# Layer 0 of a two-layer model: the products with C of four of sixteen states made by GpSimd instead of VectorE

## The chip, the cores and the metric
One core of a Trainium2 chip. The time is the device time of one execution, in microseconds.

## What is computed
Two layers on a batch of 8 sequences of 1024 tokens with 256 channels. The change lies in layer 0, in the selective scan of its Mamba block, inner width 512, 16 states:

```
def step(h, xs):
    d_t, B_t, C_t, u_t = xs
    dA = jnp.exp(d_t[..., None] * A)
    dBu = d_t[..., None] * B_t[:, None, :] * u_t[..., None]
    h = dA * h + dBu
    y_t = jnp.einsum('bdn,bn->bd', h, C_t)
    return (h, y_t)
...
y = _selective_scan(xm, delta, A, Bm, Cm, Dp)      # y + u * Dp
y = y * _silu(res)
return y @ out_proj_w.T
```

Around it stand the projection in, a convolution over four tokens, the projection out, an MLP and a mixture of experts. Layer 1 (attention with a memory term, and an MLP) is not touched.

## The kernel before
The kernel is written by hand: each engine has its own list of instructions, which it takes in order, and semaphores tie the lists. A sequence is worked in two half-sequences of 512 tokens, `j` = 0 to 15. The 512 inner channels are four tiles of 128 partitions, in two pairs `e`. For each pair the sixteen states `n` are passed, and for each state the two tiles `d`. One such (state, tile) is a step `k`: 64 steps in a half-sequence, 1024 in all; a group `g` is the two steps of one state.

In each step ScalarE writes the decay, exp(delta * A), into one of four PSUM banks (`state_bank(k)`, line 1374). GpSimd writes `drive` = delta * u * B for both tiles of a group at once (L1789), in one of three slots. VectorE scans over the 512 tokens, in place in the bank (L1578), and one scan later multiplies the states with C into `heavy` (L1560, in `weigh`). TensorE adds this piece to the y accumulators in PSUM by four transposes of 128x128 (L1056, in `add_y`). B and C of a state come by DMA over SyncE's queue (L874), spread to all partitions, into one of four slots of `bc_wide`. Four semaphores tell how far each is: `decay_done`, `driven`, `scanned`, `weighed`, and `piece_added` that a slot of `heavy` (six of them, `W_SLOTS`) is free again. A bank is written anew when its product is made; in the first half of a sequence ScalarE saves the last column to `carry` first, with which the second half starts.

At the begin of each pair VectorE multiplies the finished accumulators of the pair before with the gate (`gate_pair`, L1568), and GpSimd makes two pieces x * D into `heavy` (L1796).

Between the steps TensorE does the side work, which is everything else of layer 0 for the half-sequence after and those before: `xt` (transposes of x, L962), `xm` (projection in, L968), `cv` (convolution, L975), `res` (L981), `xd` (L986), `dl` (L991), `yt` (L996), `m` (projection out, L1002), `h` and `o` (MLP, L1007 and L1012 to L1016). A planner, `side_times`, gives each unit a step on TensorE (`PE_AT`), and its drain a step on ScalarE some six steps after the unit's end (`ACT_AT`, `put(ACT_AT, _to + 6, _unit)`) or, for `o` and two small sums, on VectorE (`DVE_AT`). The units share two PSUM banks in turn (`SIDE_BANKS`), so a unit waits until the unit two before it is drained. ScalarE's drain at step s stands behind its decay of step s - 1, and that decay waits for the product of step s - 5. On TensorE a unit of step k stands ahead of the piece of step k.

Of the kernel before, what the change touches and what calls it, by code (L numbers as in the profile page):

```python
# [15 lines left out]
ALU = mybir.AluOpType  # L16
# [106 lines left out]
W_SLOTS = 6  # L123
# [10 lines left out]

def piece_of(j, e, u, d):

    return ((j * ND + e) * (NS + 1) + u) * MD + d
# [416 lines left out]
def build(nc, x_in, w_in, p_in, moe1_in, moe2_in, resid, out):  # L554
    ctx = ExitStack()
    with ctx:
# [23 lines left out]
        def param(name):  # L580
# [7 lines left out]
        bc_wide, drive, heavy, after_scan = place(  # L588
            arena_at, ("bc_wide", [P, BC_SLOTS, 2, HALF]), ("drive", [P, DRIVE_SLOTS, MD, HALF]),
            ("heavy", [P, W_SLOTS, HALF]))  # L590
# [103 lines left out]
        piece_added = sem("piece_added")  # L694
        y_gated = sem("y_gated")
# [131 lines left out]
        def _(sp):  # L827
# [38 lines left out]
            for g in range(NH * GROUPS):  # L866
                for task in SP_AT.get(g, ()):
                    row_task(task)
                j, n = g // GROUPS, g % NS
                if g >= BC_SLOTS:  # L870
                    sp.wait_ge(driven, g - BC_SLOTS + 1)
                    sp.wait_ge(weighed, MD * (g - BC_SLOTS + 1))
                sp.wait_ge(bc_saved, 16 * (j + 1))
                sp.dma_start(bc_wide[:, g % BC_SLOTS, :, :], bc_dram[j, n:n + 1].broadcast_to([P, 2, HALF]))\  # L874
                  .then_inc(bc_in[g % BC_SLOTS], 16)
# [66 lines left out]
        def _(pe):  # L942
# [117 lines left out]

            for k in range(NH * STEPS):
                j, e, n, d = k // STEPS, k // (NS * MD) % ND, k // MD % NS, k % MD
                for unit in PE_AT.get(k, ()):
                    side(unit)
                if n == 0 and d == 0:
                    if k:
                        pe.wait_ge(y_gated, TC * (j * ND + e))
                    for i in range(MD):
                        pe.wait_ge(skip_done, (j * ND + e) * MD + i + 1)
                        add_y(j, e, 0, i)  # L1070
                pe.wait_ge(weighed, k + 1)
                add_y(j, e, n + 1, d)
# [175 lines left out]
        def _(act):  # L1248
# [112 lines left out]
            for k in range(NH * STEPS):  # L1361
                j, e, n, d = k // STEPS, k // (NS * MD) % ND, k // MD % NS, k % MD
                for task in ACT_AT.get(k, ()):
                    task_of(task)
                if n == 0 and d == 0 and e == 0:
                    act.wait_ge(softplus_done, j + 1)
                if k >= banks:
                    old = k - banks
                    act.wait_ge(weighed, old + 1)
                    if old // STEPS % NC == 0:  # L1370
                        f(carry[:, old // (NS * MD) % ND, old // MD % NS, old % MD:old % MD + 1],
                          state_bank(old)[:, HALF - 1:HALF], ACT.Copy).then_inc(carried, 1)
                        act.wait_ge(carried, old // (NC * STEPS) * STEPS + old % STEPS + 1)
                f(state_bank(k), delta[j % 2][:, e * MD + d, :], ACT.Exp,
                  scale=neg_a[:, (e * MD + d) * NS + n:(e * MD + d) * NS + n + 1]).then_inc(decay_done, 1)
# [85 lines left out]
        def _(dve):  # L1461
# [101 lines left out]
            def gate_pair(j, e):  # L1563
                dve.wait_ge(piece_added, piece_of(j, e + 1, 0, 0))
                dve.wait_ge(gate_silu, j + 1)
# [4 lines left out]
            for k in range(NH * STEPS):  # L1570
# [7 lines left out]
                V.tensor_tensor_scan(state_bank(k), state_bank(k), drive[:, g % DRIVE_SLOTS, d, :],  # L1578
# [4 lines left out]
                if k:  # L1583
                    weigh(k - 1)
# [174 lines left out]
        def _(pool):  # L1759
# [18 lines left out]

            for e in range(ND):
                row_task(("du", 0, e))  # L1780
            for g in range(NH * GROUPS):
                j, e, n = g // GROUPS, g // NS % ND, g % NS
                for task in POOL_AT.get(g, ()):
                    row_task(task)
# [153 lines left out]
```

## Time and profile before
| | us |
|---|---|
| three timed runs | 4795.88, 4803.9, 4829.52; median 4803.9 |
| profiled execution | 4818.0, its span 4815.0 |
| first scan of layer 0 to the last | 185.8 to 2320.0 in the span |
| busy in the span: TensorE, VectorE | 4237.4, 3286.6 |
| busy in the span: ScalarE, GpSimd | 2585.4, 1925.5 |

A busy time is the time in which at least one instruction of the engine is shown running. Shares over the whole span mix layer 0's prelude, its scans and layer 1, which have different limits; only the stretch from 185.8 to 2320.0 has the code of the change.

### The profile page before, as it was taken

The page shows a single profiled execution, that of the slowest core. Times are in us where ns is not written, and L with a number is a line of the kernel's source. Part 1 is how long each engine was busy: PE and PEld are TensorE (multiplying, and loading weights), DVE is VectorE, ACT ScalarE, POOL GpSimd, SP SyncE. Part 2 cuts the span into 40 slices and gives each one's busy share as a digit, 9 for nine tenths or more (in the row PEclk, how much of TensorE's full clock was granted, in tenths as well). Part 3 has the DMA queues.
Part 4 walks back from the last instruction along what each step waited for, and adds up shares of the span by engine and source line. Part 5 has one row for each costly group of instructions (what it writes and reads, how often), then busy time and mean ns, then how long its engine had stood idle before and what let it go on. Part 6 is the DMA issues. An engine that isn't in the chain of part 4 may idle for free.

```text
span 4815.0 us, 59412 instructions
## 1 busy us (share of the span) xinstructions
PE 4237.4 (88%) x20448; PEld 2458.1 (51%) x20448; DVE 3286.6 (68%) x4828; ACT 2585.4 (54%) x4047; POOL 1925.5 (40%) x1545
## 2 busy tenths in 40 slices
PE   8878888888888888887679999999999999999997
PEld 4544555555555555555444545544555445545444
DVE  0498999898999989899364564746547465564643
ACT  3465757666776767676224444444454444444444
POOL 0366666666666666666221211313122131221311
PEclk9968899898989999998779989999899989989899
DMA  2233334343433434343211121211212112121111
GB/s 95 93 131 131 122 134 144 128 149 127 149 137 127 153 124 148 132 138 136 88 38 30 21 55 21 39 33 25 48 25 51 21 28 48 22 49 26 22 39 23
DMA packets 156684, 391.58 MB, mean 81 GB/s; under 512 B 22676, under 2 KB 77284, under 8 KB 155748
## 3 DMA queue, kind: packets, MB, share of 16 engines
q1 hardware_dynamic: 156388, 387.79, 26.6%
q8 instruction: 166, 2.72, 0.2%
q14 instruction: 130, 1.06, 0.1%
HBM read 316.06 MB, written 18.87 MB: 70 GB/s over the span
## 4 chain that ended last, share of the span: by engine, by line
PE 62%; DVE 18%; ACT 9%; issue 8%; DMA 1%; POOL 1%; SPq 0%; DVEq 0%; ACTq 0%; POOLq 0%
DVE ps L1578 10%; PE ps L1135 7%; PE ps L1117 6%; PE ps L1235 5%; PE ps L1095 5%; PE ps L1228 5%; PE ps L1056 4%; DVE heavy L1560 3%; ACT L1250 3%; PE ps L1007 3%; PE ps L1160 2%; PE ps L981 2%; PE ps L1099 2%; PE ps L1166 2%; PE ps L991 2%
## 5 line engine op out<-in xcount | busy, mean ns | idle before, releaser
L1789 POOL TENSOR_TENSOR drive<-du,bc_wide 128x1024 f32<-128x1024 f32 x512 | 1207.0, 2364 | 668.2 <-DMA bc_wide<-bc_dram 560.7
L1610 DVE TENSOR_REDUCE smax<-ps 128x2 f32<-128x1024 f32 (+3 forms) x768 | 733.9, 956 | 547.2 <-PE ps L1099 369.9
L1250 ACT ACTIVATE exps<-ps 128x1024 f32<-128x1024 f32 (+3 forms) x768 | 621.0, 810 | 710.4 <-PE ps L1117 706.9
L1250 ACT ACTIVATE ps<-delta,neg_a 128x512 f32<-128x512 f32 x1024 | 701.0, 690 | 315.4 <-DVE heavy L1560 299.3
L1818 POOL TENSOR_SCALAR_AFFINE_SELECT exps<-exps 128x256 f32<-128x256 f32 x512 | 214.3, 421 | 1386.8 <-ACT exps L1250 1385.6
L1056 PEld LDWEIGHTS ps<-p_all,heavy 128*128 128x128 f32 x4352 | 552.7, 152 | 386.2 <-issue 189.6
L1056 PE MATMUL ps<-p_all,heavy 128*128 128x128 f32 x4352 | 648.7, 295 | 98.3 <-DVE heavy L1560 63.6
L1578 DVE TENSOR_TENSOR_SCAN ps<-ps,carry,drive 128x512 f32<-128x512 f32 x512 | 655.9, 1281 | 80.9 <-ACT ps L1250 80.3
L1560 DVE TENSOR_TENSOR heavy<-bc_wide,ps 128x512 f32<-128x512 f32 x1024 | 691.1, 675 | 17.8 <-PE ps L1056 17.5
L1578 DVE TENSOR_TENSOR_SCAN ps<-ps,drive 128x512 f32<-128x512 f32 x512 | 623.4, 1218 | 65.4 <-ACT ps L1250 49.8
L1095 PE MATMUL ps<-ks,qs 64*128 64x512 f32 (+3 forms) x1536 | 337.1, 436 | 79.9 <-DVE smax L1610 62.9
L1135 PE MATMUL ps<-exps,vals 128*32 128x512 f32 (+3 forms) x3072 | 385.6, 542 | 7.3 <-ACT exps L1250 3.1
L1117 PE MATMUL ps<-qs,ks 64*128 64x512 f32 (+3 forms) x1536 | 352.0, 456 | 32.7 <-ACT exps L1250 29.0
L1117 PEld LDWEIGHTS ps<-qs,ks 64*128 64x128 f32 x1536 | 152.8, 196 | 327.0 <-ACT exps L1250 143.1
L1095 PEld LDWEIGHTS ps<-ks,qs 64*128 64x128 f32 x1536 | 153.4, 196 | 315.2 <-DVE smax L1610 127.4
L1250 ACT ACT_TABLE_LOAD x235 | 301.5, 1283 | 5.0 <-PEq L1931 0.8
L1007 PE MATMUL ps<-mT,w_mlp 128*128 128x512 f32 x512 | 248.3, 610 | 56.9 <-ACT mT L1250 43.6
L1250 ACT ACTIVATE h<-ps,p_all 128x512 f32<-128x512 f32 x256 | 174.6, 682 | 202.9 <-PE ps L1228 170.1
L1016 PE MATMUL ps<-w_mlp,h 128*128 128x256 f32 x1024 | 258.3, 410 | 5.5 <-ACT h L1250 5.5
L1235 PE MATMUL ps<-g,h 128*128 128x256 f32 x1024 | 261.3, 413 | 0.0
L1228 PE MATMUL ps<-xT,g 128*128 128x512 f32 x512 | 251.9, 614 | 0.0
L975 PE MATMUL ps<-raw,taps 128*128 128x512 f32 x512 | 230.4, 592 | 0.0
(176 smaller groups left out, 5580.4 us busy)
## 6 DMA issues: line engine op xcount, KB each, us to landing
bc_wide<-bc_dram SPq DMA_DIRECT2D x512, 512.0 KB, 3.6
qs<-q_hi SPq DMA_DIRECT2D x256, 64.0 KB
ks<-k_hi SPq DMA_DIRECT2D x256, 64.0 KB, 2.4
x_row<-in_x SPq DMA_DIRECT2D x15, 1024.0 KB, 7.4
resid<-mix SPq DMA_DIRECT2D x9, 1024.0 KB, 6.8
x_row<-resid SPq DMA_DIRECT2D x9, 1024.0 KB, 5.5
xn<-resid SPq DMA_DIRECT2D x8, 1024.0 KB, 5.4
qs<-q_lo SPq DMA_DIRECT2D x128, 64.0 KB
```

Source lines behind the costliest of these rows:

```text
L1007: last = mm(bank, w_up0[:, k, m * P:(m + 1) * P], mT[:, k, :], start=(k == 0), stop=(k == KD - 1))
L1056: last = mm(acc_tile(t)[:, d * P:(d + 1) * P], heavy[:, slot, t * P:(t + 1) * P], ident, is_transpose=True, start=(u == 0 and d == 0 and t ...
L1095: last = mm(both[:, i * HALF:i * HALF + n], qs[head, slot, it * P:(it + 1) * P], ks[head, slot, ch * HALF:ch * HALF + n], start=True, stop ...
L1117: last = mm(both[:, i * HALF:i * HALF + n], ks[head, slot, jt * P:(jt + 1) * P], qs[head, slot, at:at + n], start=True, stop=True, skip_gr ...
L1135: last = mm(ps[tile:tile + VP, PV_BANK, HALF - n:], vals[:, b % 2, first:first + VP], exps[:, at + i * n:at + (i + 1) * n], start=jt < 2, ...
L1228: last = mm(bank, g1[:, k, m * P:(m + 1) * P], xT[:, b % 2, k, tokens(TC * c, HALF)], start=(k == 0), stop=(k == KD - 1))
L1235: last = mm(bank[:, 0:D], h1[:, m, tt * P:(tt + 1) * P], g2[:, m, :], start=(m == 0), stop=(m == MF - 1))
L1250: return nc.scalar.activation(out_, in_, func, **kw)
L1560: V.tensor_tensor(heavy[:, piece % W_SLOTS, :], bc_wide[:, g % BC_SLOTS, 1, :], state_bank(k), ALU.mult).then_inc(weighed, 1)
L1578: V.tensor_tensor_scan(state_bank(k), state_bank(k), drive[:, g % DRIVE_SLOTS, d, :], carry[:, e, n, d:d + 1] if j % NC else 0.0, ALU.mult ...
L1610: V.tensor_reduce(into, both, AX_X, ALU.max).then_inc(drained_v, 1)
L1789: G.tensor_tensor(drive[:, g % DRIVE_SLOTS, :, :], du[j % 2][:, e * MD:(e + 1) * MD, :], wide(bc_wide[:, g % BC_SLOTS, 0, :], MD), ALU.mul ...
```

## The change
The states n = 0, 4, 8 and 12 of each pair (`POOL_STATES`) are scanned out of the decay's bank into a buffer in SBUF, `held`, which has room for the two tiles of one state. GpSimd multiplies both tiles with C in place, by one instruction of 128x1024 (`weigh_held`), ahead of the drive of the third state after. In a sequence's first half it also copies the two last columns to `carry`, which ScalarE did. TensorE adds the eight transposes of `held` after the sixth step of each eight (`add_held`, at d = 1 of state n + 2). The scan of the next kept state waits until that is done (`held_added`). ScalarE may write a kept state's bank anew as soon as it is scanned, not weighed. SyncE waits for `held_weighed` before it overwrites such a state's C. `heavy` has four slots instead of six, which makes room for `held`; `piece_of` and `weighs_to` count the pieces and products that are left.

```diff
-W_SLOTS = 6
+W_SLOTS = 4
+POOL_STATES = (0, 4, 8, 12)
...
+            def add_held(j, e, n):
+
+                pe.wait_ge(held_weighed, pool_group(j, e, n) + 1)
+                for d in range(MD):
+                    for t in range(TC):
+                        last = mm(acc_tile(t)[:, d * P:(d + 1) * P], held[:, d, t * P:(t + 1) * P], ident,
+                                  is_transpose=True, start=False, stop=False, skip_group_check=True)
+                last.then_inc(held_added, 1)
...
-                pe.wait_ge(weighed, k + 1)
-                add_y(j, e, n + 1, d)
+                if not by_pool(n):
+                    pe.wait_ge(weighed, weighs_to(k) + 1)
+                    add_y(j, e, n + 1, d)
+                if d == MD - 1 and n >= 2 and by_pool(n - 2):
+                    add_held(j, e, n - 2)
...
-                    act.wait_ge(weighed, old + 1)
-                    if old // STEPS % NC == 0:
+                    if by_pool(old // MD % NS):
+                        act.wait_ge(scanned, old + 1)
+                    else:
+                        act.wait_ge(weighed, weighs_to(old) + 1)
+                    if old // STEPS % NC == 0 and not by_pool(old // MD % NS):
...
+                if by_pool(n) and d == 0:
+                    if pool_group(j, e, n):
+                        dve.wait_ge(held_added, pool_group(j, e, n))
+                    if j % NC:
+                        dve.wait_ge(held_carried, (j // NC * ND + e) * len(POOL_STATES) + POOL_STATES.index(n) + 1)
-                V.tensor_tensor_scan(state_bank(k), state_bank(k), drive[:, g % DRIVE_SLOTS, d, :],
+                V.tensor_tensor_scan(held[:, d, :] if by_pool(n) else state_bank(k), state_bank(k), drive[:, g % DRIVE_SLOTS, d, :],
                                      carry[:, e, n, d:d + 1] if j % NC else 0.0, ALU.mult, ALU.add)\
                     .then_inc(scanned, 1)
...
-                if k:
+                if k and not by_pool((k - 1) // MD % NS):
                     weigh(k - 1)
...
+            def weigh_held(g):
+
+                j, e, n = g // GROUPS, g // NS % ND, g % NS
+                pool.wait_ge(scanned, MD * (g + 1))
+                if j % NC == 0:
+                    G.tensor_copy(carry[:, e, n, :], held[:, :, HALF - 1]).then_inc(held_carried, 1)
+                    pool.wait_ge(held_carried, (j // NC * ND + e) * len(POOL_STATES) + POOL_STATES.index(n) + 1)
+                G.tensor_tensor(held[:, :, :], held[:, :, :], wide(bc_wide[:, g % BC_SLOTS, 1, :], MD), ALU.mult)\
+                    .then_inc(held_weighed, 1)
...
+                if g >= DRIVE_SLOTS and by_pool((g - DRIVE_SLOTS) % NS):
+                    weigh_held(g - DRIVE_SLOTS)
```

In the lists of instructions below the scan is shown as SCALAR_TENSOR_TENSOR, and in brackets stand the semaphores that an instruction waits for. VectorE around the second kept state (n = 4) of the first pair, before:

```order
L1578 SCALAR_TENSOR_TENSOR ps<-ps,drive 128x512 [waits decay_done,driven]
L1560 TENSOR_TENSOR heavy<-bc_wide,ps 128x512 [waits scanned]
L1578 SCALAR_TENSOR_TENSOR ps<-ps,drive 128x512 [waits decay_done]
L1560 TENSOR_TENSOR heavy<-bc_wide,ps 128x512 [waits piece_added,scanned]
L1578 SCALAR_TENSOR_TENSOR ps<-ps,drive 128x512 [waits decay_done,driven]
```

The same place now:

```order
L1600 TENSOR_TENSOR heavy<-bc_wide,ps 128x512 [waits piece_added,scanned]
L1624 SCALAR_TENSOR_TENSOR held<-ps,drive 128x512 [waits held_added,decay_done,driven]
L1600 TENSOR_TENSOR heavy<-bc_wide,ps 128x512 [waits scanned]
L1624 SCALAR_TENSOR_TENSOR held<-ps,drive 128x512 [waits decay_done]
L1624 SCALAR_TENSOR_TENSOR ps<-ps,drive 128x512 [waits decay_done,driven]
L1624 SCALAR_TENSOR_TENSOR ps<-ps,drive 128x512 [waits decay_done]
L1600 TENSOR_TENSOR heavy<-bc_wide,ps 128x512 [waits piece_added,scanned]
```

Two products are gone behind the two scans into `held`, and the first of these scans has one more semaphore to wait for.

TensorE in the second pair of a half-sequence, from the second `m` unit (L1002, now L1027) to the third `h` unit (L1007, now L1032) and the one after, before:

```order
L1002 MATMUL ps<-yT,w_l_52 128x512 x4
L1056 MATMUL ps<-p_all,heavy 128x128 x12
L1007 MATMUL ps<-mT,w_mlp_53 128x512 x2
L1056 MATMUL ps<-p_all,heavy 128x128 x8
L1007 MATMUL ps<-mT,w_mlp_53 128x512 x2
L1056 MATMUL ps<-p_all,heavy 128x128 x4
L1020 MATMUL ps<-row_mv,p_all 128x1
L1007 MATMUL ps<-mT,w_mlp_53 128x512 x2
L1056 MATMUL ps<-p_all,heavy 128x128 x4
L1007 MATMUL ps<-mT,w_mlp_53 128x512 x2
```

The same place now, from the kept state before it:

```order
L1091 MATMUL ps<-p_all,held 128x128 x8
L1081 MATMUL ps<-p_all,heavy 128x128 x4
L1027 MATMUL ps<-yT,w_l_53 128x512 x4
L1081 MATMUL ps<-p_all,heavy 128x128 x4
L1032 MATMUL ps<-mT,w_mlp_54 128x512 x2
L1081 MATMUL ps<-p_all,heavy 128x128 x8
L1032 MATMUL ps<-mT,w_mlp_54 128x512 x2
L1081 MATMUL ps<-p_all,heavy 128x128 x4
L1045 MATMUL ps<-row_mv,p_all 128x1
L1032 MATMUL ps<-mT,w_mlp_54 128x512 x2
L1081 MATMUL ps<-p_all,heavy 128x128 x4
L1091 MATMUL ps<-p_all,held 128x128 x8
```

The eight transposes of the kept state stand behind three `h` units and behind the transposes of the sixth step of the block.

GpSimd in the second half of a sequence, now; before, only the drives stood there:

```order
L1847 TENSOR_TENSOR drive<-du_80,bc_wide 128x1024 [waits scanned,bc_in1,du_done]
L1847 TENSOR_TENSOR drive<-du_80,bc_wide 128x1024 [waits scanned,bc_in2,du_done]
L1832 TENSOR_TENSOR held<-held,bc_wide 128x1024 [waits scanned]
L1847 TENSOR_TENSOR drive<-du_80,bc_wide 128x1024 [waits scanned,bc_in3,du_done]
L1847 TENSOR_TENSOR drive<-du_80,bc_wide 128x1024 [waits scanned,bc_in0,du_done]
```

The product of the kept state stands ahead of the drive of the third state after it, and every fifth large instruction is now such a product.

## Rows read from the trace of the kernel before

**Rows 1.** Groups by line and form, whole trace: count, busy us, mean ns, idle before.
```profile
L1560 DVE TENSOR_TENSOR heavy<-bc_wide,ps 128x512 f32<-128x512 f32 x1024 | 691.1, 675 | 17.8 <-PE ps L1056 17.5
...
L1578 DVE TENSOR_TENSOR_SCAN ps<-ps,carry,drive 128x512 f32<-128x512 f32 x512 | 655.9, 1281 | 80.9 <-ACT ps L1250 80.3 <-POOL drive L1789 0.2
...
L1789 POOL TENSOR_TENSOR drive<-du,bc_wide 128x1024 f32<-128x1024 f32 x512 | 1207.0, 2364 | 668.2 <-DMA bc_wide<-bc_dram 560.7 <-DVE ps L1578 84.2 <-issue 22.9
...
L1705 DVE TENSOR_TENSOR_SCAN gsum<-p_all,gsum,ps 112x512 f32<-112x512 f32 x48 | 61.5, 1281 | 2.1
```

**Rows 2.** Waits of VectorE from 300 to 2300 us: total us, times, longest.
```profile
DVE ps L1578 <- ACT ps L1250: 124.2, 77, 5.0
DVE heavy L1560 <- PE ps L1056: 17.5, 27, 1.8
```

**Rows 3.** Windows over the eight blocks of half-sequence 7, all engines.
```profile
1124.83:1145.20 20.37, 13.48 (x65) 10.10 (x64) 16.04 (x22) 15.30 (x22) 13.73 (x7) 0.75 0.35 121
1145.20:1160.46 15.26, 15.26 (x67) 8.89 (x66) 14.45 (x17) 8.86 (x15) 9.45 (x4) 1.00 0.58 203
1160.46:1176.58 16.12, 11.85 (x58) 7.19 (x56) 14.31 (x17) 11.12 (x14) 9.46 (x4) 1.00 0.40 135
1176.58:1194.76 18.18, 17.71 (x81) 12.53 (x82) 14.97 (x18) 13.30 (x19) 8.54 (x4) 0.91 0.34 117
1194.76:1212.36 17.60, 16.09 (x88) 11.99 (x86) 16.65 (x24) 6.47 (x10) 12.58 (x7) 1.00 0.28 100
1212.36:1231.64 19.28, 16.01 (x52) 9.73 (x52) 15.31 (x20) 12.56 (x16) 10.85 (x6) 0.73 0.38 131
1231.64:1246.41 14.77, 12.51 (x54) 7.22 (x53) 14.77 (x19) 6.96 (x11) 11.37 (x6) 1.00 0.35 120
1246.41:1261.44 15.03, 13.23 (x57) 7.65 (x56) 15.03 (x21) 9.47 (x14) 10.61 (x5) 1.00 0.41 138
```

**Rows 4.** Timeline of block 7, half-sequence 7: start us, duration us, engine, line, [idle before].
```profile
1240.49 0.67 DVE L1560 TENSOR_TENSOR heavy<-bc_wide,ps 128x512 f32<-128x512 f32 x1
...
1241.82 0.58 ACT L1250 ACTIVATE mT<-ps 128x512 f32<-128x512 f32 x1
...
1242.54 1.95 PE L1007 MATMUL ps<-mT,w_mlp 128*128 128x512 f32 x4 [2.26 <-ACT mT L1250]
...
1245.82 0.67 DVE L1560 TENSOR_TENSOR heavy<-bc_wide,ps 128x512 f32<-128x512 f32 x1
...
1246.41 1.28 DVE L1578 TENSOR_TENSOR_SCAN ps<-ps,carry,drive 128x512 f32<-128x512 f32 x1
...
1249.70 0.60 PE L1056 MATMUL ps<-p_all,heavy 128*128 128x128 f32 x4
```

**Rows 5.** Timeline of block 3, half-sequence 7.
```profile
1176.58 1.29 DVE L1578 TENSOR_TENSOR_SCAN ps<-ps,carry,drive 128x512 f32<-128x512 f32 x1 [1.81 <-ACT ps L1250]
...
1177.05 1.12 PE L996 MATMUL ps<-p_all,gate 128*128 128x128 f32 x4 [1.86 <-ACT yT L1250]
...
1183.30 0.60 PE L1056 MATMUL ps<-p_all,heavy 128*128 128x128 f32 x4
```

**Rows 6.** Timeline of TensorE in blocks 1, 6, 8 and the half-sequence after.
```profile
1150.52 1.04 PE L1056 MATMUL ps<-p_all,heavy 128*128 128x128 f32 x8
...
1216.39 1.12 PE L991 MATMUL ps<-xd_rows,w_l 64*128 64x512 f32 x2 [3.23 <-DVE mix L1503]
...
1234.06 1.48 PE L1056 MATMUL ps<-p_all,heavy 128*128 128x128 f32 x12
...
1263.30 1.91 PE L1056 MATMUL ps<-p_all,heavy 128*128 128x128 f32 x16
...
1275.07 3.30 PE L968 MATMUL ps<-xT,w_l 128*128 128x512 f32 x4 [4.66 <-ACT raw L1250]
```

**Rows 7.** Windows, columns as in 3: all of half-sequence 8.
```profile
1261.44:1392.40 130.96, 114.11 (x493) 72.49 (x492) 122.28 (x166) 100.29 (x186) 91.39 (x43) 0.92 0.43 145
```

**Rows 8.** Windows, columns as in 3: first to last scan of layer 0.
```profile
185.80:2320.00 2134.20, 1788.66 (x7648) 1142.43 (x7648) 1939.44 (x2465) 1419.32 (x2332) 1405.35 (x633) 0.88 0.39 136
```

More of the change, by code:

```diff
@@ L132, in group_of, with by_pool, pool_group, weighs_to @@
     return (j * ND + e) * NS + n
+def by_pool(n):
+    return n in POOL_STATES
+def pool_group(j, e, n):
+    return (j * ND + e) * len(POOL_STATES) + POOL_STATES.index(n)
+def weighs_to(k):
+    pairs, n, d = k // (NS * MD), k // MD % NS, k % MD
+    return (pairs * (NS - len(POOL_STATES)) + n - sum(m < n for m in POOL_STATES)) * MD + (0 if by_pool(n) else d)
 def piece_of(j, e, u, d):
-    return ((j * ND + e) * (NS + 1) + u) * MD + d
+    n = u - sum(m + 1 < u for m in POOL_STATES)
+    return ((j * ND + e) * (NS + 1 - len(POOL_STATES)) + n) * MD + d
 def side_units(i):
@@ L587, in build @@
         L0_COLS = W_AT["qk"][0]
-        bc_wide, drive, heavy, after_scan = place(
+        bc_wide, drive, heavy, held, after_scan = place(
             arena_at, ("bc_wide", [P, BC_SLOTS, 2, HALF]), ("drive", [P, DRIVE_SLOTS, MD, HALF]),
-            ("heavy", [P, W_SLOTS, HALF]))
+            ("heavy", [P, W_SLOTS, HALF]), ("held", [P, MD, HALF]))
         (w_l0, w_mlp0, taps, neg_a, ew_sum, ln_stats, ln_mv, ln_rstd, ln_shift, row_stats, row_mv, row_q, carry, tail,
@@ L694, in build @@
         piece_added = sem("piece_added")
+        held_weighed = sem("held_weighed")
+        held_carried = sem("held_carried")
+        held_added = sem("held_added")
         y_gated = sem("y_gated")
@@ L870, in _ @@
                 if g >= BC_SLOTS:
-                    sp.wait_ge(driven, g - BC_SLOTS + 1)
-                    sp.wait_ge(weighed, MD * (g - BC_SLOTS + 1))
+                    old = g - BC_SLOTS
+                    sp.wait_ge(driven, old + 1)
+                    if by_pool(old % NS):
+                        sp.wait_ge(held_weighed, pool_group(old // GROUPS, old // NS % ND, old % NS) + 1)
+                    else:
+                        sp.wait_ge(weighed, weighs_to(MD * (old + 1)))
                 sp.wait_ge(bc_saved, 16 * (j + 1))
@@ L1368, in _ @@
                     old = k - banks
-                    act.wait_ge(weighed, old + 1)
-                    if old // STEPS % NC == 0:
+                    if by_pool(old // MD % NS):
+                        act.wait_ge(scanned, old + 1)
+                    else:
+                        act.wait_ge(weighed, weighs_to(old) + 1)
+                    if old // STEPS % NC == 0 and not by_pool(old // MD % NS):
                         f(carry[:, old // (NS * MD) % ND, old // MD % NS, old % MD:old % MD + 1],
                           state_bank(old)[:, HALF - 1:HALF], ACT.Copy).then_inc(carried, 1)
-                        act.wait_ge(carried, old // (NC * STEPS) * STEPS + old % STEPS + 1)
+                        act.wait_ge(carried, old // (NC * STEPS) * weighs_to(STEPS) + weighs_to(old % STEPS) + 1)
                 f(state_bank(k), delta[j % 2][:, e * MD + d, :], ACT.Exp,
@@ L1564, in gate_pair @@
                 dve.wait_ge(piece_added, piece_of(j, e + 1, 0, 0))
+                dve.wait_ge(held_added, len(POOL_STATES) * (j * ND + e + 1))
                 dve.wait_ge(gate_silu, j + 1)
```

## The prediction

> **What bounds the kernel now.** Read the whole-trace groups first, then the windows of layer 0, then VectorE's waits, and last the order of time inside one block of steps. Layer 0's scan part lasts 2134.2 us of the span and VectorE is busy 1939.4 of it, TensorE 1788.7, GpSimd 1405.4 [rows 8]. It is VectorE that sets the pace: a scan of 1281 ns and a product of 675 ns per step, pipelined, 1024 times [rows 1]. It waits 124.2 us for ScalarE's decays and only 17.5 us for TensorE [rows 2]. So a product taken from VectorE looks like time gained.
>
> The second thing to see is how far TensorE runs behind VectorE, and why. Number the steps of a half-sequence 0 to 63 (two tiles per state, sixteen states, two pairs) and cut them into eight blocks of eight; each block begins with a state that the change gives to GpSimd. At the end of block 7 VectorE starts the first scan of block 8 at 1246.41. The transposes of step 53 (the sixth of block 7) end at 1249.70 + 0.60 = 1250.30 [rows 4]: TensorE is 3.9 us late against that scan. This lag is not a heap of old work. TensorE had sat idle for 2.26 us until 1242.54, waiting for ScalarE to drain mT; the drain at 1241.82 stands behind the decay that needed the product started at 1240.49 [rows 4]. The side work (convolution, projections, MLP) uses two banks in turn, and its drains are tied to ScalarE's place in the steps, which is tied to VectorE's. At present this costs nothing, since six pieces may wait in heavy. Block 3 shows the same: idle 1.86 us before 1177.05 for yT, step 21 ended at 1183.90, while the first scan of block 4 began at 1176.58, 7.3 us earlier [rows 5].
>
> **The change part by part.** (1) Removed from VectorE: 256 products. A product takes the engine 0.59 us from start to start (1245.82 to the scan at 1246.41, [rows 4]), so a block gets 1.19 us shorter on VectorE's side and all 128 blocks 151 us. The Trainium skill (VectorE: DVE Perf Modes, "The DRAIN you can't avoid") says that the next operation does not start until the pipe has emptied; here the scan starts before the 0.67 us product has ended, so the measured 0.59 stands. By that rule the saving would be 256 times the mean 675 ns, 173 us.
>
> (2) The scans of the kept states write SBUF instead of PSUM. The scan of layer 1 that reads PSUM and writes SBUF, 512 elements, takes 1281 ns, as the one here does [rows 1]: taken at nothing, between 0 and the 0.06 us by which the two groups of scans might differ, 512 times, 30 us at most either way.
>
> (3) Added to GpSimd: 256 products of 128x1024. The form stands in the trace as drive, 2364 ns [rows 1]: 605 us. For half of them a copy of 128x2 as well, not in the trace; above nothing and below a quarter of that operation, 0 to 0.6 us each, taken at 0.2: 26 us. GpSimd is idle for 2134.2 - 1405.4 = 729 us there [rows 8], so it fits, with 98 us to spare. The product is issued ahead of the drive three states later, so it delays that drive by 2.4 us, and it frees its bc_wide slot for SyncE's queue, which stands behind it. The kept product comes about 2.4 us after its scans, while TensorE asks for it after five more steps; I take no wait from this.
>
> (4) TensorE: as many transposes as before. Eight of a kept state come at once behind the sixth step of the block, 1.04 us by the row of eight [rows 6].
>
> (5) The new wait, the one that decides. There is one held buffer. The first scan of a block waits until TensorE has added the kept state of the block before, and in TensorE's queue those eight transposes stand behind the sixth step's side work and transposes. Behind the waiting scan are all scans and products of VectorE; ScalarE's decays and GpSimd's drives wait for those. So a block cannot be shorter than: the time from its first scan to the end of its sixth step on TensorE, plus 1.04 for the eight transposes, plus 0.1 for two semaphores, less the 1.19 by which VectorE reaches the releasing point earlier. That is 0.05 less than the distance measured now. It holds where a wait inside the block made TensorE late, since then nothing is inherited; where TensorE was late from an earlier block the wait itself has cleared that, and I take VectorE's own time, the block less 1.19.
>
> The eight blocks of half-sequence 7 last 20.37, 15.26, 16.12, 18.18, 17.60, 19.28, 14.77 and 15.03 us, 136.6 in all [rows 3]. Block by block, after:
> - Block 3: 1183.90 - 1160.46 = 23.4 in place of 16.1 [rows 3, 5].
> - Block 6: TensorE idles 3.23 us for VectorE's mix, then works partly at 1.2 GHz, the lower of its two levels (the granted clock of the block is 0.73 on average); step 45's transposes end at 1234.06 + 1.04 = 1235.10, so 22.7 in place of 19.3 [rows 3, 6].
> - Block 7: 1250.30 - 1231.64, 18.6 in place of 14.8 [rows 3, 4].
> - Block 8: step 61 ends at 1263.30 + 1.04 = 1264.34, 17.9 in place of 15.0 [rows 3, 6].
> - Block 1: step 5 ends at 1150.52 + 0.60 = 1151.1, 26.2 us after the block's begin, against 19.2 by VectorE alone [rows 3, 6]. Part of this lag comes from the Gelu, which would start earlier once TensorE hands over a shorter queue. I take 22, nearer the low end, for 20.4 now.
> - Block 2: TensorE is busy all of its 15.26 us, with inherited work [rows 3]; I take 15.0.
> - Blocks 4 and 5 by VectorE's own time: 17.0 and 16.4 [rows 3].
> Sum 153.0 against 136.6, 16.4 more. Half-sequence 8 (131.0 us, [rows 7]) belongs to the other kind, in which the next sequence is normalised; there TensorE idles 4.66 us for raw in block 1 [rows 6], the same pattern, and I take 16 for it as well. The first and the last half-sequence have little side work: there VectorE's own gain stands, 8 times 1.19, 9.5 each. In all 14 times 16 less 19, 205 us. The profiled execution took 4818 us, which makes 5023; it was 14 above the median of the three timed runs, so against 4804 I say **5009 us**, 4% slower.
>
> heavy with four slots in place of six adds nothing to this: the product that would wait for a slot needs a step that the held wait has asked for already, or one that TensorE finishes early in the block. Alone it would cost, since the lag of 3.9 to 7.3 us above is more than a window of two states.
>
> **The rivals.** Rival A, faster: the lag is old work and TensorE catches up as soon as VectorE asks. Then a block lasts the longer of VectorE's own time and TensorE's busy time: 19.2, 15.3, 14.9, 17.7, 16.4, 18.1, 13.6, 13.8 [rows 3], 129.0, so 7.6 less per half-sequence and 122 in all: 4682 us. It speaks for it that TensorE is busy for 1788.7 of 2134.2 us only [rows 8]; against it are the idle stretches of 1.9 to 4.7 us right ahead of the late steps [rows 4 to 6]. It decides once TensorE has its sixth step done within 0.7 us of its product, which is what the two steps of VectorE that follow (1.78 us) leave beside 1.04 us of transposes.
>
> Rival B, GpSimd's products are what TensorE and the drives wait for: then of the 151 us all but a little is given back, and GpSimd, with 98 us to spare over 128 blocks, stalls VectorE in the blocks that also hold du and the joins. At one product's 2.36 us in each of 64 blocks, 151 us, this comes out level: 4804 us. Against it is that a drive is ready early in most blocks and GpSimd idles before it.
>
> Rival C, no lag is cleared: each block lasts as long as the distance measured now, inherited work included. Blocks 2 and 4 would show the lags of blocks 1 and 3 again, some 4 us each, and block 1 its 26.2: 12 more per half-sequence, 168 in all, 5177 us.
>
> Rival D, the change does not do what it says, the wait being met by an earlier release. The order shows TensorE's eight transposes behind the sixth step in every block, so I leave it little.
>
> **How the numbers follow.** Forecast 0.72, from 4883 (the lag counts for less than half: 14 times 7 less 19 is 79) to 5121 (block 1 at its upper end and 4 us more in block 2: 14 times 24 less 19 is 317); rival A 0.06; rival B and D together 0.12, 4780 to 4880; rival C 0.10. The range of 4860 to 5130 leaves out A, most of B and C. Within 1% is about what a measurement of this kernel can tell from no change, that is 4756 to 4852: 0.08. Faster 0.06, slower 0.86.
>
> **What would show it.** Right: the scans into held wait for TensorE's transposes of held, over 300 us in total, in blocks 1, 3, 6, 7 and 8, hardly in 5; ScalarE's stalls of VectorE shrink below 124 us; TensorE's idle waits for ScalarE's drains grow; the products and scans keep 675 and 1281 ns; layer 1 is unchanged. Wrong: held waits below 100 us (A), or waits of TensorE for held_weighed and of scans for drive (B). The forecast would fail most easily through the assumption that ScalarE's drains come no earlier relative to the steps than they do now.

## The result, and the profile after

The changed kernel takes **5038.8 us** (median of 4 runs, 5034.0 to 5055.0), the kernel before 4810.6 in the same session (4 runs, 4795.9 to 4829.5): a ratio of 1.048, 95% interval 1.043 to 1.052. The forecast was 5009 us, with a range of 4860 to 5130. The profiled execution has a span of 5037.9 us.

First the windows: the scan part of layer 0 (first scan to last) and the stretch of layer 1 from its first to its last gate scan, of the kernel after and then of the kernel before. (The first window of the kernel after runs to the end of its last scan, 1.3 us more than to its start.) Columns: window, length, busy time and count of TensorE, its weight loads, VectorE, ScalarE and GpSimd, granted clock, DMA share, GB/s.

```profile
186.80:2577.40 2390.60, 1877.86 (x7642) 1184.44 (x7643) 1785.49 (x2209) 1392.88 (x2204) 1708.03 (x825) 0.85 0.36 122
2728.60:4778.60 2050.00, 1939.05 (x10651) 1026.70 (x10649) 1189.28 (x2060) 958.17 (x1405) 442.85 (x795) 0.92 0.17 33
```
```profile
185.80:2318.70 2132.90, 1787.55 (x7644) 1141.71 (x7644) 1938.14 (x2464) 1419.32 (x2332) 1405.35 (x633) 0.88 0.39 137
2473.50:4559.40 2085.90, 1965.28 (x10669) 1037.71 (x10667) 1187.97 (x2061) 961.38 (x1409) 448.20 (x798) 0.91 0.17 33
```

VectorE did lose its work: 1785 us busy, 153 fewer. And yet layer 0's scan part is longer, 2389.3 us from first to last scan start against 2132.9, **256.4 more**. Layer 1 gives 36 of it back in this pair of profiles, but nothing there was changed: over the fourteen traces of this study, one of each kernel, that stretch lasts from 2043 to 2094 us. It goes with TensorE's granted clock in it: the two longest (2094 and 2086, the second that of the kernel before) have 0.901 and 0.909, the two shortest (2043 and 2050, the second that of the kernel after) 0.927 and 0.921. What sets that clock is open, and so is how much of the 36 us belongs to the kernels and how much to these two executions. A difference in the whole time of some 25 us can lie outside the changed code, so the lengths of the scan part are given below where it matters.

Next the costliest groups, with the idle time of the engine ahead of each; they answer to [rows 1].

```profile
L1600 DVE TENSOR_TENSOR heavy<-bc_wide,ps 128x512 f32<-128x512 f32 x768 | 516.0, 672 | 145.5 <-PE ps L1081 145.1
L1624 DVE TENSOR_TENSOR_SCAN held<-ps,carry,drive 128x512 f32<-128x512 f32 x128 | 163.6, 1278 | 202.2 <-PE ps L1091 190.0 <-POOL drive L1847 10.6 <-ACT ps L1287 1.6
L1624 DVE TENSOR_TENSOR_SCAN held<-ps,drive 128x512 f32<-128x512 f32 x128 | 155.8, 1218 | 170.4 <-PE ps L1091 156.3 <-POOL drive L1847 12.6 <-ACT ps L1287 1.3
L1832 POOL TENSOR_TENSOR held<-held,bc_wide 128x1024 f32<-128x1024 f32 x128 | 301.2, 2353 | 174.3 <-DVE held L1624 169.1
L1847 POOL TENSOR_TENSOR drive<-du,bc_wide 128x1024 f32<-128x1024 f32 x512 | 1203.9, 2359 | 333.9 <-DMA bc_wide<-bc_dram 137.6 <-issue 134.8 <-DVE ps L1624 57.0
L1830 POOL COPY carry<-held 128x2 f32<-128x2 f32 x64 | 12.0, 187 | 122.0 <-DVE held L1624 121.9
```

The durations are what they were: 672 ns a product, 1278 ns a scan, also into SBUF; GpSimd's new product takes 2353 ns. The idle time is new: 346 us ahead of scans into `held`, for the transposes of the kept state (L1091; this is called the held wait below), and 145 us ahead of VectorE's own products, for those of pieces (L1081). ([rows 2] had 17.5 of the latter.)

The eight blocks of half-sequence 7, to be laid beside [rows 3]:

```profile
1225.55:1248.14 22.59, 16.18 (x75) 11.10 (x73) 14.65 (x19) 14.61 (x20) 16.66 (x9) 0.85 0.41 140
1248.14:1262.02 13.88, 13.88 (x59) 7.88 (x57) 13.10 (x14) 7.28 (x12) 10.59 (x5) 1.00 0.44 147
1262.02:1285.31 23.29, 15.53 (x64) 9.77 (x62) 13.21 (x15) 13.51 (x18) 14.27 (x7) 0.78 0.27 93
1285.31:1300.62 15.31, 14.73 (x80) 11.51 (x78) 13.43 (x15) 11.20 (x14) 8.51 (x4) 1.00 0.37 137
1300.62:1319.18 18.56, 14.70 (x66) 10.11 (x64) 15.53 (x22) 5.96 (x9) 17.04 (x9) 0.82 0.32 118
1319.18:1339.63 20.45, 18.46 (x70) 11.24 (x70) 14.18 (x17) 12.24 (x15) 12.72 (x6) 0.83 0.31 103
1339.63:1361.16 21.53, 15.51 (x53) 8.56 (x50) 13.85 (x16) 7.74 (x12) 16.21 (x7) 0.84 0.28 98
1361.16:1380.14 18.98, 14.57 (x57) 8.36 (x58) 13.54 (x18) 11.22 (x16) 8.42 (x4) 0.91 0.32 111
```

And block 7 in order of time (start, duration, engine, line, idle before), to be laid beside [rows 4]:

```profile
1339.63 1.28 DVE L1624 TENSOR_TENSOR_SCAN held<-ps,carry,drive 128x512 f32<-128x512 f32 x1 [3.84 <-PE ps L1091]
...
1347.28 0.67 DVE L1600 TENSOR_TENSOR heavy<-bc_wide,ps 128x512 f32<-128x512 f32 x1
...
1348.61 0.58 ACT L1287 ACTIVATE mT<-ps 128x512 f32<-128x512 f32 x1
...
1349.34 3.75 PE L1032 MATMUL ps<-mT,w_mlp 128*128 128x512 f32 x4 [5.60 <-ACT mT L1287]
...
1359.49 0.60 PE L1081 MATMUL ps<-p_all,heavy 128*128 128x128 f32 x4
...
1359.92 1.04 PE L1091 MATMUL ps<-p_all,held 128*128 128x128 f32 x8
1361.16 1.28 DVE L1624 TENSOR_TENSOR_SCAN held<-ps,carry,drive 128x512 f32<-128x512 f32 x1 [5.58 <-PE ps L1091]
```

Read it as a ring. The scan at 1339.63 had waited, so ScalarE's decays start late, and so do the product at 1347.28 and the drain of mT tied to it (1348.61). TensorE has cleared its queue by then and stands idle for 5.60 us. It comes back at the lower of its two levels, 1.2 GHz: in the window from 1349.30 to 1353.10 the granted clock is 0.50, and four matmuls take 3.75 us where [rows 4] have 1.95. The sixth step ends at 1360.09, the eight transposes behind it at about 1361, and the scan that begins the next block has waited 5.58 us. The block lasts 21.5 us in place of 14.8. The window of those slow matmuls, columns as above:

```profile
1349.30:1353.10 3.80, 3.77 (x6) 1.62 (x7) 3.44 (x4) 1.38 (x2) 3.80 (x3) 0.50 0.40 146
```

Over the whole scan part TensorE's idle time that ends with something from ScalarE grew from 209 to 304 us.

### The profile page after: what moved, and what is told of

It reads as the page before. It is cut to its first block, busy times and chain, and to the rows that moved or that the text cites. A ratio compares the mean times of both kernels' runs of the same rounds, so it can differ in the third digit from the quotient of the medians.

```text
span 5037.9 us, 59155 instructions
## 1 busy us (share of the span) xinstructions
PE 4304.2 (85%) x20448; PEld 2492.2 (49%) x20448; DVE 3136.0 (62%) x4572; ACT 2558.2 (51%) x3919; POOL 2224.1 (44%) x1737
## 4 chain that ended last, share of the span: by engine, by line
PE 65%; DVE 14%; issue 9%; ACT 9%; DMA 2%; POOL 1%; DVEq 0%; SPq 0%; ACTq 0%; POOLq 0%
PE ps L1172 6%; PE ps L1272 5%; PE ps L1154 5%; PE ps L1265 5%; PE ps L1132 5%; PE ps L1081 5%; DVE ps L1624 4%; PE ps L1041 3%; DVE heavy L1600 3%; PE ps L1032 3%; PE ps L1197 2%; ACT L1287 2%; PE ps L1006 2%; PE ps L1136 2%; DVE smax L1656 2%
## 5 line engine op out<-in xcount | busy, mean ns | idle before, releaser
L1847 POOL TENSOR_TENSOR drive<-du,bc_wide 128x1024 f32<-128x1024 f32 x512 | 1203.9, 2359 | 333.9 <-DMA bc_wide<-bc_dram 137.6
L1081 PE MATMUL ps<-p_all,heavy 128*128 128x128 f32 x3328 | 546.9, 304 | 173.4 <-DVE heavy L1600 130.5
L1081 PEld LDWEIGHTS ps<-p_all,heavy 128*128 128x128 f32 x3328 | 446.8, 158 | 435.7 <-issue 194.2
L1600 DVE TENSOR_TENSOR heavy<-bc_wide,ps 128x512 f32<-128x512 f32 x768 | 516.0, 672 | 145.5 <-PE ps L1081 145.1
L1624 DVE TENSOR_TENSOR_SCAN ps<-ps,carry,drive 128x512 f32<-128x512 f32 x384 | 485.9, 1276 | 33.6 <-ACT ps L1287 30.2
L1624 DVE TENSOR_TENSOR_SCAN ps<-ps,drive 128x512 f32<-128x512 f32 x384 | 462.8, 1215 | 59.8 <-ACT ps L1287 39.3
L1032 PE MATMUL ps<-mT,w_mlp 128*128 128x512 f32 x512 | 277.3, 674 | 129.0 <-ACT mT L1287 87.7
L1832 POOL TENSOR_TENSOR held<-held,bc_wide 128x1024 f32<-128x1024 f32 x128 | 301.2, 2353 | 174.3 <-DVE held L1624 169.1
L1132 PEld LDWEIGHTS ps<-ks,qs 64*128 64x128 f32 x1536 | 153.0, 196 | 308.8 <-DVE smax L1656 128.5
L1624 DVE TENSOR_TENSOR_SCAN held<-ps,carry,drive 128x512 f32<-128x512 f32 x128 | 163.6, 1278 | 202.2 <-PE ps L1091 190.0
L1624 DVE TENSOR_TENSOR_SCAN held<-ps,drive 128x512 f32<-128x512 f32 x128 | 155.8, 1218 | 170.4 <-PE ps L1091 156.3
```

What stands on the lines that cost most here:

```text
L1032: last = mm(bank, w_up0[:, k, m * P:(m + 1) * P], mT[:, k, :], start=(k == 0), stop=(k == KD - 1))
L1081: last = mm(acc_tile(t)[:, d * P:(d + 1) * P], heavy[:, slot, t * P:(t + 1) * P], ident, is_transpose=True, start=(u == 0 and d == 0 and t ...
L1132: last = mm(both[:, i * HALF:i * HALF + n], qs[head, slot, it * P:(it + 1) * P], ks[head, slot, ch * HALF:ch * HALF + n], start=True, stop ...
L1600: V.tensor_tensor(heavy[:, piece % W_SLOTS, :], bc_wide[:, g % BC_SLOTS, 1, :], state_bank(k), ALU.mult).then_inc(weighed, 1)
L1624: V.tensor_tensor_scan(held[:, d, :] if by_pool(n) else state_bank(k), state_bank(k), drive[:, g % DRIVE_SLOTS, d, :], carry[:, e, n, d:d ...
L1832: G.tensor_tensor(held[:, :, :], held[:, :, :], wide(bc_wide[:, g % BC_SLOTS, 1, :], MD), ALU.mult)\
```

## The experiments

Twelve kernels, in three batches; each batch has its own runs of the kernel before (medians 4806 to 4811). "VectorE's waits" below are its idle time around the scan part of layer 0, by what ended it; those for `drive` include one of 9 us or so ahead of the very first scan, in every kernel. A drain "two steps earlier" stands behind the decay of two steps before in ScalarE's list.

Four kernels leave out part of the computation, with as many instructions as before. The ones with six slots and `held`, and with two held buffers (`e2`, `e3`), use one half of layer 0's first MLP weight twice, the one with both (`e4`) one half of each MLP weight, which makes room in SBUF; `e6` leaves out most of GpSimd's product. Their times are compared, their results are not the reference's.

### The two resources apart

Slots of pieces alone, in the kernel before:

```
-W_SLOTS = 6
+W_SLOTS = 4
```

> The kernel before, with four slots for the pieces (heavy) in place of six; nothing else. A product then waits until TensorE has added the piece three steps before. Theory H (the wait for held is what costs, and it costs because TensorE's side work is forced to run 4 to 7 us behind by the drains): the same lag must now cost here as well, without any held buffer. By the rows of before, the product at the begin of the next block would wait about 4.7, 6.1, 2.3, 2.7 and 1.7 us in blocks 1, 3, 6, 7, 8, some 13 to 17 us per half-sequence, 4990 us, plus or minus 40. Rival S (the two lost slots are the whole cost of the change): 5040 or more, since here all products stay on VectorE. Rival N (slots hardly matter): 4810 to 4840.

Measured: 4980.7 us, 1.035 (1.031 to 1.038 of the time before), as expected: 171 us for two buffers. The kernel before needs the six: VectorE waits 316 us for pieces, against 17.5.

The other way round, the changed kernel with its six slots back:

```
-W_SLOTS = 4
+W_SLOTS = 6
...
```

> The changed kernel with six slots for the pieces again, so that only the held buffer with its wait is left of the change. The room comes from leaving out one half of the first weight of layer 0's MLP (both products over the halves of the channels use the same half), with as many instructions as before. Theory H: the held wait asks for a later step of TensorE than any slot, so 5000 to 5040 us, hardly less than the changed kernel's 5039. Rival S (lost slots): back to 4700 to 4810.

Measured: 5052.2, 1.049 (1.046 to 1.053), 12 us above the expected range; the slots bring nothing. VectorE's waits (who, for whom, us in total, times, longest) show why: the wait for pieces is gone and the held wait has taken it over, 495 us in place of 346 and 145.

```profile
DVE held L1624 <- PE ps L1091: 494.6, 102, 11.8
DVE ps L1624 <- ACT ps L1287: 76.6, 39, 5.0
```

Then a second held buffer, so that a block's first scan waits for the state of two blocks ago (the lines that pick the buffer, and those of the weight, are left out here):

```
...
-            ("heavy", [P, W_SLOTS, HALF]), ("held", [P, MD, HALF]))
+            ("heavy", [P, W_SLOTS, HALF]), ("held", [P, 2, MD, HALF]))
...
-                    if pool_group(j, e, n):
-                        dve.wait_ge(held_added, pool_group(j, e, n))
+                    if pool_group(j, e, n) > 1:
+                        dve.wait_ge(held_added, pool_group(j, e, n) - 1)
...
```

> The changed kernel with two held buffers in turn, four slots for the pieces, and half of the MLP's first weight left out to make room (as many instructions as before). A scan of a kept state waits for the state two blocks back. Theory H in its plain form: the held waits vanish (329 us to under 20), but the four slots then ask for TensorE's steps three steps back: waits of the products for pieces rise from 136 to 200 to 300 us, time 4900 to 4980. Rival (held alone is the cost, the slots take no part): 4680 to 4750.

Measured: **4780.5**, 0.994 (0.993 to 0.996), so 258 us less than the changed kernel, and far below the 4900 to 4980 that I expected. The held wait carries the whole loss. What I had wrong is the price of the slots beside it: I took e1's cost to stand here too. But VectorE waits 145 us for pieces, less than half of e1's 316. With every fourth state kept out of `heavy`, four pieces reach further back in time at most places of a block. The places show it: in e1 the products of the first, third, fifth and seventh step of a block wait 40, 31, 145 and 100 us in all, here almost the whole wait (143 us) stands at the seventh. Its waits, of the kernel with two held buffers:

```profile
DVE heavy L1600 <- PE ps L1081: 145.1, 68, 7.9
DVE ps L1624 <- POOL drive L1848: 71.4, 71, 3.1
DVE ps L1624 <- ACT ps L1287: 65.1, 41, 4.6
```

Both at once (edits of the two kernels above together):

> The changed kernel with two held buffers and six slots; to make room, half of each of the MLP's two weights in layer 0 is left out (the other half is used twice, with as many instructions as before). Theory H: with the lag allowed again, VectorE's gain shows: 4680 to 4740 us, waits of VectorE for TensorE under 60 us in layer 0. Rival P (TensorE's or ScalarE's own pace is the next limit, so that the products were not worth moving): 4790 to 4830. Rival G (GpSimd is too slow for the products): waits of scans for drive over 100 us and 4800 or more.

Measured: 4748.4, 0.986 (0.983 to 0.990), a little above the expectation. Its scan part lasts 2080.2 us against 2132.9. With room for TensorE's whole lag, the 151 us taken from VectorE come to 62 us. New beside the kernel before are the waits for `drive`, 106 us against 16; those for decays are 116 us against 130.

### The place of the eight transposes

```
-                if d == MD - 1 and n >= 2 and by_pool(n - 2):
-                    add_held(j, e, n - 2)
+                if d == MD - 1 and n >= 1 and by_pool(n - 1):
+                    add_held(j, e, n - 1)
```

> The changed kernel; TensorE adds the kept state behind the fourth step of a block, not the sixth (at d = 1 of state n + 1 instead of n + 2). Theory H (what counts is how late in TensorE's queue the eight transposes stand): the wait of the next kept scan loses the side work of steps 5 and 6, so the held waits fall from 329 us to 60 to 150 us, but four slots still bind: 4950 to 5000 us. Rival G (GpSimd's product is late): TensorE now waits for it, the time stays at 5040 or rises.

Measured: 4817.6, 1.002 (1.000 to 1.004): 221 us back from two lines changed, more than expected and without any more memory. The held wait falls from 346 to 17.5 us. TensorE's work is the same, only its order is not. It is the place in TensorE's queue, not the one buffer as such, that costs. VectorE's waits in this kernel:

```profile
DVE heavy L1600 <- PE ps L1081: 132.3, 61, 8.3
DVE ps L1624 <- POOL drive L1847: 94.0, 72, 3.1
...
DVE held L1624 <- PE ps L1091: 17.5, 55, 1.1
```

### Is GpSimd's product what is waited for? (rival B)

```
-                G.tensor_tensor(held[:, :, :], held[:, :, :], wide(bc_wide[:, g % BC_SLOTS, 1, :], MD), ALU.mult)\
+                G.tensor_tensor(held[:, :, 0:2], held[:, :, 0:2], wide(bc_wide[:, g % BC_SLOTS, 1, 0:2], MD), ALU.mult)\
```

> The changed kernel; GpSimd multiplies only the first two tokens of each kept state with C, so the product of the other 510 is left out. All waits and transposes stay. Theory H: GpSimd's 605 us of products lie beside other work, so 5020 to 5045 us. Rival G (GpSimd's products or the drives and B/C loads behind them bound blocks): 4940 or less, with the scans' waits for drive (47 us) gone.

Measured: 5056.2, 1.052 (1.048 to 1.056), 11 us above the expected range. GpSimd's products take 26 us in all in place of 301, and the kernel is no faster (the held wait is 359 us). Rival B is out: its price does not lie on the path of the changed kernel.

### Half as many kept states

```
-POOL_STATES = (0, 4, 8, 12)
+POOL_STATES = (0, 8)
```

> The changed kernel with two kept states of sixteen (0 and 8) in place of four; one held buffer, four slots. The wait for held then comes ten steps behind the add. Theory H: held waits below 10 us; what is left is the cost of four slots less 128 products on VectorE (75 us): 4880 to 4950 us. Rival (every kept state costs by itself, through GpSimd or the semaphores): half of the 228 us, 4925 with held waits still there; if the slots cost nothing, 4735.

Measured: 4912.2, 1.022 (1.018 to 1.027), as expected. With sixteen steps between two kept states no scan waits for one (no such line among VectorE's waits), but the loss is halved, not gone: the four slots now cost about what e1 leads one to expect, 171 us less 75 for the 128 products taken away (measured: 106). VectorE's waits in this kernel:

```profile
DVE heavy L1600 <- PE ps L1081: 262.0, 127, 7.3
DVE ps L1624 <- POOL drive L1847: 76.8, 60, 3.1
```

### Where TensorE's lag comes from

The prediction put the lag down to ScalarE's drains, tied to its place in the steps. So the drains of a unit are put two steps earlier, in the changed kernel:

```
-        put(ACT_AT, _to + 6, _unit)
+        put(ACT_AT, _to + 4, _unit)
```

> The changed kernel; ScalarE drains each side unit of layer 0 four steps after its planned end on TensorE instead of six. Theory H says TensorE is late because its units wait for drains that stand late in ScalarE's list: two steps (3.6 us) less in most blocks, held waits down by a half, 4880 to 4950 us. Rival T (TensorE is late with work, not for drains): 5030 to 5100, since ScalarE now waits for TensorE and holds up the decays.

Measured: 4826.7, 1.004 (1.002 to 1.006), 212 us less than the changed kernel and below the 4880 to 4950 expected. The held wait is 138 us in place of 346, the wait for pieces 11 in place of 145, and TensorE's idle time that ends with something from ScalarE 105 in place of 304. The same edit in the kernel before is the control:

> The kernel before with side units drained four steps after their planned end instead of six: the control. Theory H: with six slots TensorE's lag costs nothing there, and ScalarE now waits a little more for TensorE: 4800 to 4850 us. Rival (the earlier drains are worth something by themselves, and what they did for the changed kernel is not about its new waits): 4700 or less.

Measured: 4742.8, 0.985 (0.983 to 0.987), well below the 4800 to 4850 expected. So the kernel before gains 68 us by it as well, and 144 of the 212 come on top in the changed kernel. Here I was wrong on the kernel before: its 17.5 us of products waiting for TensorE did not tell what a shorter lag is worth. Of the 68 us its scan part has 56 (2076.8 us against 2132.9). VectorE's idle time in it falls from 195 to 150 us (its waits of `gate` for TensorE from 30 to 4, those of products from 18 to nothing, while those for decays rise from 130 to 143), and its busy time by 11 us, of which 7 are in small operations that take a scalar and two tensors (from 21 to 14 us in all). Why these get shorter stays open.

Slots and drains together, in the kernel before:

```
-W_SLOTS = 6
+W_SLOTS = 4
...
-        put(ACT_AT, _to + 6, _unit)
+        put(ACT_AT, _to + 4, _unit)
```

> The kernel before with four slots for the pieces and drains four steps after the planned end; all products on VectorE. Theory H: the 171 us that four slots cost are the same forced lag, so the earlier drains give most of them back: 4820 to 4870 us, waits of products for pieces from 316 us to under 80. Rival (four slots are too few for TensorE's uneven side work as such): 4940 to 4990.

Measured: 4793.2, 0.996 (0.995 to 0.998), below the 4820 to 4870 expected, though products still wait 91 us for pieces and not under 80. Two slots cost 50 us with early drains and 171 with late ones: the same buffer has another price as soon as the lag is shorter.

Then e5's and e8's edits together:

> The changed kernel with both cures that need no memory: the kept state is added behind the fourth step of a block, and side units are drained four steps after their planned end. Theory H: held waits under 20 us and waits for pieces under 40, as each cure took one of the two away; left are ScalarE's and GpSimd's stalls (158 and 72 us with the earlier drains, 64 and 125 with the earlier add). 4690 to 4760 us, faster than before. Rival: both cures remove the same waits and GpSimd or ScalarE bounds what is left, 4800 to 4830.

Measured: **4739.2** (4734.0 to 4741.6), 0.984 (0.982 to 0.986). It is faster than both kernels, as expected, but it is level with the kernel before with the same drains (4738.3 to 4746.5). And the drains halfway, one step earlier only, with e5's edit:

> As the first of this set, with drains five steps after the planned end. If ScalarE's stalls (waiting for TensorE) are what the earlier drains cost, this lies below the version with four by 5 to 20 us; if TensorE's lag still matters there, above it by 10 to 40.

Measured: 4795.0, 0.996 (0.995 to 0.998), 56 us above the kernel with two steps, more than the 10 to 40 expected. The scan part has 45 us of that; layer 1, which is the same code, lasts 19 us longer in this profile. The waits for pieces are 71 us here against 8 there.

What the change is worth where no wait of its own is left is read from VectorE's waits in the kernel with early transposes and early drains, and then in the kernel before with early drains:

```profile
DVE ps L1624 <- ACT ps L1287: 116.0, 76, 4.3
DVE ps L1624 <- POOL drive L1847: 88.0, 102, 3.1
...
DVE held L1624 <- POOL drive L1847: 38.1, 44, 9.4
```
```profile
DVE ps L1578 <- ACT ps L1250: 143.0, 91, 4.2
...
DVE ps L1578 <- POOL drive L1789: 11.9, 2, 9.4
```

The waits for `drive` are 126 us where the kernel before has 12. VectorE is busy 139 us less and idle 124 us more, so its scan part is 15 us shorter (2062.0 against 2076.8); the medians of the runs differ by 4. By these waits it is the supply of `drive` that takes most of the gain back.

It does so in two ways. The product stands ahead of the drive of the third state after it, and the scans of that state wait 33 us for it. But the waits at the next kept state (29 us, without the very first scan) and at the state after it, whose drive stands behind the late one (45 us), have another origin, a row of three steps that the lines of GpSimd show (with them the load on SyncE's queue and the scan that waits):

```profile
1203.31 2.36 POOL L1832 TENSOR_TENSOR held<-held,bc_wide 128x1024 f32<-128x1024 f32 x1
...
1205.62 2.36 POOL L1847 TENSOR_TENSOR drive<-du,bc_wide 128x1024 f32<-128x1024 f32 x1
1205.73 4.55 SPq L899 DMA_DIRECT2D bc_wide<-bc_dram  x3
...
1209.77 2.36 POOL L1847 TENSOR_TENSOR drive<-du,bc_wide 128x1024 f32<-128x1024 f32 x1 [1.78 <-issue]
...
1212.16 1.22 DVE L1624 TENSOR_TENSOR_SCAN held<-ps,drive 128x512 f32<-128x512 f32 x1 [0.49 <-POOL drive L1847]
```

The slot with the kept state's C is free only when GpSimd's product has ended (1205.67). The load of the next kept state's B and C goes into that slot: it is issued at 1205.73 and takes 3.9 us to land (median of 512). Only then can the drive of that state begin, and GpSimd is not busy ahead of it but idle for 1.78 us ("issue": the profile names nothing that it waits for, but the time of the landing does). Over the scan part GpSimd stands idle ahead of 105 of the 128 drives of kept states, 196 us in all, and in 103 of these the drive starts less than 0.3 us after its load has landed. So the price is that of a late release of a slot as much as that of the engine's time. No run takes either away in this kernel: that VectorE would then keep its 151 us is not shown.

## Why the prediction was right

**The mechanism** was the one named in step 5, the held wait. It was forecast at over 300 us, in blocks 1, 3, 6, 7 and 8 and hardly in 5. It measures 346; over the 14 half-sequences in the middle the first scan of the block that follows stalls for 5.3 us on the mean after block 1, 4.1 after 3, 4.0 after 6, 4.5 after 7, 2.4 after 8, 1.6 after 4, which the forecast did not name, and 1.0 or less after 2 and 5. Taking the wait's cause away in three ways (a second buffer, an earlier place, earlier drains) gave 258, 221 and 212 us back, the last with 68 that the kernel before gains too.

**Block by block**, half-sequence 7 was forecast at 22, 15.0, 23.4, 17.0, 16.4, 22.7, 18.6 and 17.9 us; it has 22.6, 13.9, 23.3, 15.3, 18.6, 20.5, 21.5 and 19.0: 154.6 in all against 153.0. That the sum is so close is partly luck: block 7 is 2.9 and block 5 2.2 longer than forecast, block 6 is 2.2, block 4 1.7 and block 2 1.1 shorter. Reading the distance from a block's first scan to the end of its sixth step on TensorE out of the profile before was good to 0.1 us in block 3, and 2.9 short in block 7. There the forecast assumed that the drains come no earlier relative to the steps. They did (9.0 us after the block's begin, 10.2 before), but TensorE had idled 5.6 us for them and worked at the lower clock afterwards, which made four matmuls alone 1.8 us longer. Step 5 had no such term. Its 0.1 us for two semaphores was small: from the end of the eight transposes to the scan they release it is 0.20 us (median of 98).

**The sum.** The 14 middle half-sequences were taken at 16 each and measure 16.8 each on the mean (235.0 us in all; 10.9 in the third, 19.2 in the twelfth). The first and the last were taken at 9.5 less each, 19 together, "the first and the last half-sequence have little side work", and that step failed: they measure 12.9 and 8.5 more, 21 together, so this term alone is 40 us off. Both have held waits as well (12.5 and 16.4 us), and the first waits 9.5 us for pieces. VectorE's waits in the first half-sequence after:

```profile
DVE held L1624 <- PE ps L1091: 12.5, 4, 4.9
DVE held L1624 <- POOL drive L1847: 11.9, 3, 9.5
DVE heavy L1600 <- PE ps L1081: 9.5, 2, 6.4
```

Little side work on the mean still makes single units late, and one late unit is enough. So layer 0's scan part grew by 256 us where I had 205, 51 too few. The medians differ by 228 only, so the error in the time itself is 30 us. The two profiles differ by 223, as what stands outside the scan part, layer 1 above all, is 33 us shorter in the one after. The forecast took that rest as unchanged; that it came to the forecast's help is luck.

**heavy with four slots "adds nothing to this"**: e2 bears it out in time (6 slots in the changed kernel, 13 us slower rather than faster), though not by the reason given. VectorE's products do wait 145 us for pieces, more than half of it (77 us) at the end of block 3. What the slots would save, the held wait takes, as both wait for the same late TensorE. "Alone it would cost" is right: 171 us.

**Steps 1 to 4** stand: VectorE is busy 153 us less (151 forecast from start to start, 173 by the full duration), the product of 672 ns still takes 0.58 to 0.59 us from start to start, the scans into SBUF keep 1278 and 1218 ns. GpSimd's products are 301 us for 128 of them, and not the 605 us written down: step 3 counted 256 products of 128x1024, but one instruction serves both tiles of a state. GpSimd is thus busy 1708 us and not 2036; the slip changed nothing in the sum, only left GpSimd less room than it has. The copy takes 187 ns (0.2 forecast), 64 times. ScalarE's stalls of VectorE fell from 124 to 63 us (from 300 to 2500 us of the span), as said. Step 3 named the slot of `bc_wide` that is freed late, but took no wait from it: it costs little in the changed kernel, and shows once the held wait is gone.

**The rivals.** A (TensorE catches up, 4682 us) is refuted by 346 us of held waits where it allows 100: the lag is made anew by the drains, and falls with them in e8. B (level, by GpSimd) is refuted by e6 for this kernel; waits for `drive` turn up as soon as the held wait is gone (125 us in e5, 126 in e9, which is level with its control), in part by GpSimd's product and in part by the load behind it, which the rival did not name. C (no lag cleared, 5177) is refuted by blocks 2 and 4, which are 1.4 and 2.9 us shorter than before: the wait does clear the lag. D (the wait met by an earlier release) is refuted by the held waits.

## What to carry to other kernels

Before moving work off the busiest engine, look at how far behind it the next engine runs at each place and what that distance is made of: here TensorE ran up to 7.3 us late because the drains of its side work were tied to steps, and a buffer that asks for it sooner costs the distance, once per block. A buffer's depth and a queue position are the same currency: two changed lines in TensorE's queue gave back 221 us where a second buffer gave 258, and four slots cost 171 us or 50, according to where the drains stood. And time taken from an engine is worth only as much as its other suppliers are early: of 151 us, 4 to 62 were left. When work moves to another engine, follow every slot whose release moves with it: here a slot that was freed later held up a load, and the load the next drive.

## What the runs showed of the hardware

GpSimd's in-place product of 128x1024 f32 takes 2353 ns, as its product into another buffer does (2359), and it does not slow VectorE beside it: with GpSimd busy 1708 us in place of 1405, the products are 672 ns (675 before) and the scans 1276 (1281). Its 128x2 copy costs 187 ns. TensorE's granted clock in the scan part fell from 0.88 to 0.85 with the longer idle stretches, so that a wait of another engine is paid a second time: behind 5.60 us of idle time matmuls took 0.94 us at a granted clock of 0.50, where the same ones took 0.49 at 1.00 before. And layer 1, unchanged in all fourteen kernels, lasts from 2043 to 2094 us, by and large the longer the lower its granted clock (0.927 in the shortest, 0.901 in the longest).
